# The convolution's weights of a gated-delta-rule kernel: one DMA of 64 rows of 2 KB and four TensorE transposes in place of one DMA of 8192 pieces of 16 bytes

## The reference, cut to what matters

```
xn = _layernorm(x)                                   # x: (2, 512, 256)
qkvz = xn @ W_qkvz; ba = xn @ W_ba
mixed = concat(q, k, v)                              # 8192 channels
y = silu(conv_general_dilated(mixed, conv_w, causal, depthwise))   # conv_w: (8192, 4)
o = chunk_gated_delta_rule(q, k, v, g(ba), beta(ba))
x = x + (o * silu(z), normalized) @ W_out + ternary_ffn(xn)
```

## Time and profile before

| | us |
|---|---|
| median of three runs | 1959.18 |
| lowest, highest | 1953.77, 1960.43 |
| profiled execution, its own time | 1964.37 |
| span in its trace | 1962.2 |
| TensorE busy | 1572.7 (80%) |
| VectorE busy | 1034.9 (53%) |
| ScalarE busy | 826.6 (42%) |
| GpSimd busy | 507.0 (26%) |

### The profile page before, as it was taken

How to read it: one execution, slowest core, us unless ns; L and a number is a source line. 1 busy time by engine, 2 the same in 40 slices (tenths; PEclk the granted TensorE clock), 3 DMA queues, 4 the chain that set the end, 5 groups by cost and what they waited for, 6 DMA issues and landing times. The chain is left out here.

```text
span 1962.2 us, 40518 instructions
## 1 busy us (share of the span) xinstructions
PE 1572.7 (80%) x16552; PEld 1126.9 (57%) x16552; DVE 1034.9 (53%) x1962; ACT 826.6 (42%) x1599; POOL 507.0 (26%) x558
## 2 busy tenths in 40 slices
PE   2165887878878798888888788888969995888999
PEld 2033565656656565665656566665646673454665
DVE  7754646556464655547465554746553314266234
ACT  2143445444445444444544444444434312566300
POOL 5730222312231231313222231222213323310100
PEclk9577899989999998998989898999989997799999
DMA  5221101111010111101111110111030002000200
GB/s 144 79 68 24 36 13 26 47 23 28 10 36 24 26 42 28 26 13 34 26 25 36 35 25 13 33 27 25 12 90 12 1 1 60 1 2 1 65 1 22
DMA packets 187735, 60.89 MB, mean 31 GB/s; under 512 B 153024, under 2 KB 180288, under 8 KB 187296
## 3 DMA queue, kind: packets, MB, share of 16 engines
q1 hardware_dynamic: 169216, 50.30, 11.3%
q10 hardware_dynamic: 18336, 8.01, 1.6%
HBM read 39.21 MB, written 19.07 MB: 30 GB/s over the span
## 5 line engine op out<-in xcount | busy, mean ns | idle before, releaser
L1099 POOL TENSOR_TENSOR og<-og,sz 128x256 f32<-128x256 f32 x128 | 92.9, 726 | 757.3 <-DVE og L1041 532.3
L506 PE MATMUL banks<-wv,xT 128*128 128x512 f32 x256 | 139.9, 698 | 78.6 <-DVE Yv L892 54.1
L892 DVE SCALAR_TENSOR_TENSOR Yv<-banks,cwall,Yv 128x1022 f32<-128x1022 f32 (+2 forms) x96 | 122.3, 1274 | 82.2 <-ACT Yv L736 81.5
L506 PEld LDWEIGHTS banks<-wv,xT 128*128 128x128 f32 x256 | 54.3, 223 | 149.4 <-issue 149.4
L506 PE MATMUL banks<-wqk,xT 128*128 128x512 f32 x256 | 123.7, 628 | 20.2 <-DVE Yk L892 19.6
L869 ACT ACTIVATE V<-banks,skd 128x128 f32<-128x128 f32 x192 | 59.9, 363 | 165.7 <-PE banks L677 165.4
L646 PE MATMUL banks<-wz,xT 128*128 128x256 f32 x512 | 125.5, 389 | 1.4 <-DVE yacc L1061 1.4
L715 PE MATMUL banks<-wo,oT 128*128 128x256 f32 x512 | 122.9, 383 | 0.8 <-ACT oT L885 0.8
L646 PEld LDWEIGHTS banks<-wz,xT 128*128 128x128 f32 x512 | 100.7, 199 | 23.7 <-issue 9.8
L1070 POOL TENSOR_TENSOR E<-E,nsk 128x1024 f32<-128x1024 f32 x32 | 60.9, 1925 | 165.2 <-DVE nsk L919 161.1
L715 PEld LDWEIGHTS banks<-wo,oT 128*128 128x128 f32 x512 | 93.8, 190 | 14.8 <-issue 1.9
(11 more groups left out here) (368 smaller groups left out, 3717.2 us busy)
## 6 DMA issues: line engine op xcount, KB each, us to landing
cm_d<-CM SPq DMA_DIRECT2D x32, 256.0 KB, 3.9
wqk<-in_L_attn_W_qkvz SPq DMA_DIRECT2D x8, 512.0 KB, 4.7
wv<-in_L_attn_W_qkvz SPq DMA_DIRECT2D x8, 512.0 KB, 3.8
wz<-in_L_attn_W_qkvz SPq DMA_DIRECT2D x16, 256.0 KB, 2.8
wo<-in_L_attn_W_out SPq DMA_DIRECT2D x16, 256.0 KB, 3.1
blk<-cm_d SPq DMA_DIRECT2D x128, 16.0 KB, 1.8
t_d<-tb SPq DMA_DIRECT2D x16, 128.0 KB, 1.7
u_d<-ub SPq DMA_DIRECT2D x16, 128.0 KB, 1.8
```

The costliest lines, as they stand in the source:

```text
L506: ins = pe.matmul(bank[b][:, :], xT[:, d, b * S + of_batch, :], w[:, d, :], start=(d == 0), stop=(d == KD - 1))
L892: v.scalar_tensor_tensor(y, pair[0][:, :, 0:T - j], conv_w(k, t)[:, 3 - j:4 - j], y, ALU.mult, ALU.add).then_inc(s["tap"].sem, 1)
L1099: pool.tensor_tensor(og[:, n, :, :], og[:, n, :, :], sz[q % 2][:, b, :].rearrange("p (h d) -> p h d", h=VR), ALU.mult).then_inc(s["osz"].s ...
```

## The change

The weights are read as `"(h p) j -> h p j"`: 64 partitions, each a contiguous row of 512 floats, into `cwr`, the first 64 partitions of the scratch tile `t512` (in the listing below `t`). The DMA has a semaphore of its own, `pcw`, and `psmall` now counts three DMAs. TensorE turns the four taps, each a [64, 128] slice with a stride of four floats, into columns of `bank[3]`, and VectorE copies the 256 columns into `cwall`, reordering them. The first tap waits for that copy (`cwe`) in place of `psmall`.

```diff
-        act.dma_start(m["cwall"][:, :, :], a["L0_attn_conv_w"].rearrange("(h p) j -> p h j", p=P)).then_inc(s["psmall"].sem, 16)
+        act.dma_start(cwr[:, :, :], a["L0_attn_conv_w"].rearrange("(h p) j -> h p j", p=P)).then_inc(s["pcw"].sem, 16)
...
         yield START["pba"]
+        pe.wait_ge(*s["pcw"]())
+        pe.wait_ge(*s["const"]())
+        for j in range(4):
+            ins = pe.transpose(bank[3][:, j * 64:(j + 1) * 64], cwr[:, :, j], c["ident"][0:64, 0:64])
+        ins.then_inc(s["cwp"].sem, 1)
         pe.wait_ge(*s["pxT"]())
...
         yield START["ba"]
+        v.wait_ge(*s["cwp"]())
+        v.tensor_copy(m["cwall"][:, :, :], bank[3][:, 0:256].rearrange("p (j h) -> p h j", j=4)).then_inc(s["cwe"].sem, 1)
...
         if k == 0 and t == 0:
-            act.wait_ge(*s["psmall"]())
+            act.wait_ge(*s["cwe"]())
```

More of the change, by code:

```diff
@@ L135, in psum @@
     return [pair[i // 2][:, i % 2, :] for i in range(8)], pair
-PREP = {"px": -B, "pwba": -1, "psmall": -4, "iota": 2, "const": 20, "pln": 4, "prs": 1, "pxTp": NT, "pxT": NT, "pba": 1, "pgate": 9, "pact": 4, "pgsum": 1, "pgT": 1, "pgp": 5, "pg_d": -6}
+PREP = {"px": -B, "pwba": -1, "psmall": -3, "pcw": -1, "cwp": 1, "cwe": 1, "iota": 2, "const": 20, "pln": 4, "prs": 1, "pxTp": NT, "pxT": NT, "pba": 1, "pgate": 9, "pact": 4, "pgsum": 1, "pgT": 1, "pgp": 5, "pg_d": -6}
 def constants(nc):
@@ L151, in constants, with prep @@
     return c
-def prep(s, a, c, bank, m, wide, more, small, ints):
+def prep(s, a, c, bank, m, wide, more, small, ints, rows):
     xa, xT, tab, half = m["yacc"], m["xT"], m["tab"], c["half"]
@@ L160, in prep @@
     dtb, alog, pf, pg = (small[:, 128 + i * 32:160 + i * 32] for i in range(4))
+    cwr = rows.rearrange("p (c j) -> p c j", j=4)
     ta, tm, sp_, g, gc, gT = (more[:, i * W:(i + 1) * W] for i in range(6))
@@ L429, in gdn @@
     over_group = lambda t, g: t[:, g % 2, :].unsqueeze(2).to_broadcast([P, 16, GR64])
-    start = prep(s, a, c, bank, m, line(E), line(CM), line(Td), line(P4))
+    start = prep(s, a, c, bank, m, line(E), line(CM), line(Td), line(P4), t512[0:(2 + VR) * HK, :])
     at = lambda k: FIRST if k == 0 else FINAL if k == LAST else AT
```

## The result

The changed kernel takes 1972.15 us in the median of 9 runs (1962.30 to 1981.05), the kernel before, run beside it, 1954.44 us (9 runs). The ratio is 1.0085, 95% interval 1.0058 to 1.0113. (Ratios and intervals here stand as they are on record; they are not quotients of the two medians.) Run once more later on, it gave 1.0057 (1.0042 to 1.0072). The forecast was 1956.5, within 0.3% of no change, so it is wrong, and in the direction that had the smallest chance.

The account below looks back on a forecast made before the run. It took the preparation, with ACT held 20.18 us in a DMA issue, to be on the path that sets the end; 2.7 us off the median of 1959.18 gave 1956.5 us, range 1950.0 to 1963.5.

Parts of the forecast that it names:

- ACT's queue: ACT's five early DMA issues end by about 3.3 us, the bias's falling from 20.18 to about 0.46; first cast at 13.6.
- the sum: The preparation's end moves 1.4 to 2.74 us earlier, taken as 2.7, and the shift reaches the kernel's end.
- Ternary and `xT` chain: Preparation behind `xn`: DVE's first ternary reduction starts 2.74 us earlier (22.70), ACT's first `xT` copy 1.86 us earlier (23.45).
- Four turns: On PE ahead of the `ba` projection: cost 0.89 to 1.11 us, less the gap 0.37 to 0.59, taken as 0.45.
- Copy: DVE's copy of 128 x 256 out of PSUM takes 0.42 us, hidden in a gap before ACT's table.
- Where they meet: On DVE, line 232, set by POOL on the ternary chain, ends at 36.88 and not 39.62: 2.74 us earlier.
- A: The forecast itself: whole kernel 2 to 3 us faster, 1956.5 us; chance 0.60.
- B: The release of ACT doesn't come or doesn't reach the end: 0 to 1.4 us gained, about 1958.5; chance 0.14.
- D: Heads: two groups fewer at the low TensorE clock, 9.5 us faster, 1949.7, or one fewer, 1953.1; chance 0.16.
- C: Heads: the preparation's new end puts two more groups at the low TensorE clock, net +4.1 us, 1963.3; chance 0.10.

Follow-up runs that it names:

- the filler kernel: The kernel before with 18 waits on an already passed count on TensorE, 9 further instructions and nothing of the change: 1971.38 us, ratio 1.0061.
- At an equal place: The changed kernel with 495 idle waits on TensorE, its stream 256 instructions (one whole block) longer than the kernel before: 1955.93 us, ratio 0.9994.
- The kernel with the end given back: The changed kernel with two further VectorE memsets (2.2 us) delaying the preparation, so the heads start when they did before: 1974.27 us, ratio 1.0094.
- the kernel with the DMA moved: The kernel before with its 8192-piece DMA issued behind ACT's first cast with its own semaphore, no turns or copy: 1958.27 us, ratio 0.9997.
- +9 to +52: Kernels with 9 to 52 more TensorE instructions than the kernel before, with or without the change: ratios 1.0043 to 1.0094.
- +0, +5 and +64: Kernels with that many more TensorE instructions than the kernel before: +0 ratio 1, +5 without the change 1.0009, +64 without 1.0019 and with 1.0022.

## Why the prediction was wrong, point by point

**ACT's queue: right.** Five issues of 0.50 to 0.63 us, the last ends at 3.74 (forecast 3.3); the cast stands at 15.41, its data 1.8 us later than the 13.6 of the sum. It is hidden all the same, with 7.6 us to spare.

**Ternary and `xT` chain: right, less 0.5 to 0.65.** Both started from `xn`, which the sum held fixed at 22.67. It ends at 23.31. The first tile of x comes later, the first statistics wait for it. Before and after:

```profile
6.98 2.38 DVE L213 BATCH_NORM_STATS2 bn<-yacc 128x6 f32<-128x256 f32 x7 [0.39 <-DMA yacc<-in_L_attn_x]
```
```profile
7.63 1.73 DVE L214 BATCH_NORM_STATS2 bn<-yacc 128x6 f32<-128x256 f32 x5 [1.03 <-DMA yacc<-in_L_attn_x]
```

The term that I left out is what ACT's loads, now all issued by 3.74 us, do to the loads of x: 0.65 us. It is no chance of one execution: in the kernels that hold ACT as before, the first statistics start at 6.9 to 7.0 us, and in those with the change at 7.6 to 8.0. With it the reduction starts at 23.23 (2.21 earlier, not 2.74) and the first copy at 24.09 (1.22, not 1.86).

**Four turns: right in kind, priced too high.** 0.75 us from the first's start to the last's end, 0.68 until the `ba` projection starts; the forecast said 0.89 to 1.11 less the gap. The projection starts 1.13 us earlier where the first copy of `xT` gained 1.22, so the turns cost the chain 0.09 us and not 0.45. **Copy: right**, 0.41 us and hidden (35.06 to 35.47, ACT's table comes at 35.85).

**Where they meet: right.** Line 232, now 235, takes 0.68 us, no longer 1.76, and ends at 37.41 in place of 39.62: 2.21 earlier, the ternary chain's gain, although its neighbour on the table's side gained 1.13. The last ternary turn is 2.22 earlier where the sum said 2.7.

**The step that failed** is the sentence behind the sum: "All behind it waits on semaphores of work that moves as well, the loads have long landed, and so the shift reaches the end". The semaphores did move. What did not move along is the division of TensorE's own instructions into blocks, which I had costed at nothing because the four turns were priced by their duration alone. Their number, 9 with the wait, costs 0.6% (the filler kernel), some 12 us, against 2.2 gained. The runs show that cost and that it goes with the place; how it comes about they show in part only. At an equal place the ratio of the changed kernel is 0.9994 (0.9973 to 1.0014), which holds the forecast's 0.9986 and also no gain; a gain of 2 us is below what the runs can tell.

**The rivals.** A, the forecast, held up to the start of the heads and not to the end. B fell: the release reached the heads. D, faster by the clock, didn't come. C had the right sign, and its price of 3.4 us for a group at the lower clock fits the traces (8 steps of 0.85 in place of 0.43 us), but its start was wrong: it took the preparation's end as what moves the clock. The kernel with the end given back is as slow (1.0094), and the stretch that it looked at is not the worse one: 110 to 120 us reads 0.68 after against 0.53.

```profile
110.00:120.00 10.00, 8.58 (x34) 4.67 (x33) 6.18 (x7) 5.28 (x8) 4.61 (x2) 0.68 0.14 52
```

"Against: nothing in the order of the heads changes" was true and no argument, since their place in the stream changed.

## What to carry to other kernels

In a long unrolled program, an edit near the start moves everything behind it against the blocks in which the instructions come in. In this kernel, whose heads run through 128 short multiplications in little over 1 us, that decides over half a per cent, so here a difference of that size proves nothing about the edit. Put in a filler of the same number of instructions without the edit, and the edit with a filler up to the next whole period, before believing either.

## What the runs showed of the hardware that I had not expected

- TensorE pauses for 1 to 3 us at block crossings in runs of 32x32 multiplications, 23 to 29 pauses over 0.4 us and 46 to 56 us in all, in every one of the twenty profiled executions. The Trainium skill, "Runtime: NRT & Kernel Launch", section "Instruction fetch mechanics", says that the cost of crossing a 16 KiB boundary is mostly hidden. For the 133 crossings of this kernel that holds in number, and not for the fifth of them that pauses, nearly all in or just behind short work.
- A DMA of 8192 pieces of 16 bytes is itself issued quickly; it is the next issue on that queue that stands. Behind ACT's first cast it took 0.39 us to issue and landed in 10.2 us, with nothing behind it until 30.78 us. The timeline and the landing (KB, us) of the kernel with the DMA moved:

```profile
15.50 0.39 ACTq L1127 DMA_DIRECT2D cwall<-in_L_attn_conv_w  x1
...
30.78 0.39 ACTq L1131 DMA_DIRECT2D A<-in_L_ffn_w  x1
```
```profile
cwall<-in_L_attn_conv_w ACTq DMA_DIRECT2D x1, 128.0 KB, 10.2
```

- A pause ends 1.2 to 1.7 us after the end of the 16 KB packet that brings the block, in all 499 pauses of over 0.7 us at crossings. What shows as "issue" idle can be this wait.
- The mean granted clock of an execution says little; the time that TensorE is busy at the lower level says more. In the heads it runs from 158 to 200 us over the twenty executions, and the heads' busy time follows it.
- Open stays how 2.3 us more of pauses become 12: why at +9 to +52 TensorE is busy at the lower level for longer, and not busy for longer beyond the pauses, than at +0, +5 and +64. The runs show that it goes with the place, and not by which step.
